# A pool of seven PSUM banks for the second attention of a two-attention layer

## The reference, cut to what matters

```python
def _mha(xq, xk, xv, Wq, bq, Wk, bk, Wv, bv, Wo, bo, causal):
    q = jnp.einsum('bsd,hde->bhse', xq, Wq) + bq[None, :, None, :]
    k = jnp.einsum('bsd,hde->bhse', xk, Wk) + bk[None, :, None, :]
    v = jnp.einsum('bsd,hde->bhse', xv, Wv) + bv[None, :, None, :]
    scale = 1.0 / jnp.sqrt(jnp.asarray(HD, q.dtype))
    scores = jnp.einsum('bhqe,bhke->bhqk', q, k) * scale
    if causal:
        ...
    w = jax.nn.softmax(scores, axis=-1)
    out = jnp.einsum('bhqk,bhke->bhqe', w, v)
    out = out.transpose(0, 2, 1, 3).reshape(out.shape[0], out.shape[2], D)
    return out @ Wo + bo
h = _mha(x, x, x, ..., causal=True)
out = _mha(h, encoder_k, encoder_v, ..., causal=False)
```

## Time and profile before

| | us |
|---|---|
| median of three runs | 3932.46 (3927.11 to 3933.49) |
| the profiled execution | 3969.99 |
| its span | 3968.2 |
| second attention, first scores to last unit | about 3451 to 3894 of the span |
| TensorE busy over the span | 3345.0 (84%) |
| DVE busy | 2614.8 (66%) |
| ACT busy | 1963.7 (49%) |

### The profile page before, as it was taken

The page is one execution under the profiler, slowest core; times in us unless marked ns, Lnnn a source line. Parts: engine busy times, 40 slices in busy tenths (PEclk is TensorE's granted clock), DMA queues, the critical chain, the costliest instruction groups (busy, mean ns, idle before and its releaser), DMA issues. The chain is left out here.

```text
span 3968.2 us, 96220 instructions
## 1 busy us (share of the span) xinstructions
PE 3345.0 (84%) x40498; PEld 2324.9 (59%) x40498; DVE 2614.8 (66%) x4510; ACT 1963.7 (49%) x3525; POOL 1266.7 (32%) x842
## 2 busy tenths in 40 slices
PE   7566797999999997756549668999999979999996
PEld 4445665777777776721123345766666656666664
DVE  5124375666666666279977778888888854666663
ACT  1122344555555554459950335665656652356552
POOL 1101303555555552400021336665556621000000
PEclk9577888999999998887878889999999995799996
DMA  1021401000000000800000221111111101000000
GB/s 40 6 63 57 157 1 39 1 10 1 10 1 1 1 1 20 274 28 1 1 5 2 62 71 32 53 49 45 44 53 38 30 15 39 9 19 20 11 1 11
DMA packets 88726, 131.40 MB, mean 33 GB/s; under 512 B 18450, under 2 KB 60106, under 8 KB 87532
## 3 DMA queue, kind: packets, MB, share of 16 engines
q1 hardware_dynamic: 85292, 119.03, 10.5%
q0 software_dynamic: 3008, 6.23, 0.4%
HBM read 86.63 MB, written 10.94 MB: 25 GB/s over the span
## 5 line engine op out<-in xcount | busy, mean ns | idle before, releaser
L2774 POOL TENSOR_TENSOR wide_probs<-wide_probs,wide_factor 128x1024 f32<-128x1024 f32 x128 | 239.6, 1893 | 311.1 <-ACT wide_factor L2735 311.1
L175 POOL TENSOR_TENSOR model_Y<-model_Y,model_X 128x512 f32<-128x512 f32 x12 | 15.2, 1266 | 963.7 <-POOLq L66 963.7
L2731 ACT ACTIVATE wide_probs<-wide_ps_s,wide_nm 128x1024 f32<-128x1024 f32 (+1 forms) x256 | 237.2, 926 | 172.5 <-DVE wide_nm L2816 152.8
L2281 ACT ACTIVATE narrow_probsT<-narrow_ps_t 128x512 f32<-128x512 f32 (+1 forms) x448 | 228.5, 565 | 181.5 <-PE narrow_ps_t L2185 178.8
L2811 DVE TENSOR_REDUCE wide_nm<-wide_ps_s 128x1 f32<-128x1024 f32 x128 | 155.9, 1219 | 193.6 <-PE wide_ps_s L2617 193.6
L3921 POOL TENSOR_TENSOR local_turn<-local_turn 128x1024 f32<-128x1024 f32 x96 | 226.7, 2368 | 158.7 <-DVE local_turn L3979 158.2
L2336 DVE TENSOR_REDUCE narrow_part<-narrow_ps_s 128x1 f32<-128x512 f32 x384 | 237.3, 682 | 57.9 <-PE narrow_ps_s L2168 57.9
L2185 PE MATMUL narrow_ps_t<-narrow_Q,second_KQ 32*128 32x256 f32 (+1 forms) x1664 | 261.8, 401 | 0.2 <-ACT narrow_probsT L2281 0.2
L3135 DVE TENSOR_TENSOR bonds_strain<-peri_in_moved 128x1664 f32<-128x1664 f32 (+3 forms) x128 | 257.0, 2083 | 1.0 <-PEq L66 1.0
L3186 PE MATMUL bonds_ps<-bonds_act_of,bonds_out 128*32 128x448 f32 (+3 forms) x1024 | 153.5, 696 | 117.9 <-ACT bonds_act_of L3159 83.9
L2629 PE MATMUL wide_ps<-model_ident,wide_probs 128*128 128x128 f32 (+1 forms) x1664 | 239.0, 274 | 10.8 <-DVE wide_probsT L2821 9.1
(11 more groups left out here) (643 smaller groups left out, 8433.9 us busy)
## 6 DMA issues: line engine op xcount, KB each, us to landing
moe_w<-in_L_ffn_w SPq DMA_DIRECT2D x62, 512.0 KB, 4.9
local_V<-local_V SPq DMA_DIRECT2D x96, 128.0 KB
e_wqkv<-in_L_ffn_qkv SPq DMA_DIRECT2D x6, 1536.0 KB, 6.8
local_V<-local_V SPq DMA_DIRECT2D x144, 64.0 KB
context_rows<-in_ctx SPq DMA_DIRECT2D x8, 768.0 KB
e_keys<-in_ctx_T SPq DMA_DIRECT2D x6, 800.5 KB, 4.9
e_source<-in_ctx_T SPq DMA_DIRECT2D x4, 800.5 KB, 4.5
second_source<-in_ctx_T SPq DMA_DIRECT2D x4, 800.5 KB, 6.4
```

What stands on the lines that cost most here:

```text
L2281: act.activation(probsT[0:high, c % PROBS, h, 0:wide], bank[0:high, 0:wide], ACT.Exp).then_inc(t_taken_act.sem, 1)
L2731: act.activation(probs[:, n % 2, h, lo:hi], ps_s[h][:, 0:hi - lo], ACT.Exp, bias=nm[:, n % 2, h, 2 * half:2 * half + 1], scale=1.0, accum_ ...
L2774: pool.tensor_tensor(v, v, factor[:, n // 4 % 2, j:j + 1].broadcast_to([P, CUT]), ALU.mult).then_inc(lowered[i].sem, 1)
```

## The change

The seven banks become one list. A loop ahead of the kernel walks the plan with assumed times (0.4 us per unit on TensorE, 1.2 for `times`, 2 us from issue to release, 0.6 per unit on DVE, 0.5 on ACT) and gives each unit the bank that it expects to be free first. Each unit waits for the last user of its bank, whichever engine empties that. The plan itself, the instructions and their operands' shapes are as before. Where `a.context` is false the banks and waits come out as before. At every place where a bank is asked for, `wait_bank_s` and `wait_bank_t` become `empty`, and `full_s` and `full_t` become `full`.

```diff
@@ narrow_attention: set-up, after the plan is sorted
     SB, TBK = 4, 3
+    BANKS = SB + TBK
+
+    slot_of, turn_of, last_in = {}, {}, {}
+    users = [[] for _ in range(BANKS)]
+    free, issued, dve_through, act_through = [0.0] * BANKS, 0.0, 0.0, 0.0
+    for e in plan:
+        if e[0] == "times":
+            issued += 1.2
+        if e not in s_rank and e not in t_rank:
+            continue
+        if a.context:
+            k = min(range(BANKS), key=lambda k: free[k])
+        else:
+            k = s_rank[e] % SB if e in s_rank else SB + t_rank[e] % TBK
+        issued = max(issued + 0.4, free[k])
+        if e in s_rank:
+            free[k] = dve_through = max(dve_through + 0.6, issued + 2)
+        else:
+            free[k] = act_through = max(act_through + 0.5, issued + 2)
+        slot_of[e], turn_of[e] = k, len(users[k]) + 1
+        last_in[e] = users[k][-1] if users[k] else None
+        users[k].append(e)
...
-        ps_s = [place.psum(f"ps_s{i}", [P, BANK]) for i in range(SB)]
-        ps_t = [place.psum(f"ps_t{i}", [P, BANK]) for i in range(TBK)]
+        ps = [place.psum(f"ps{i}", [P, BANK]) for i in range(BANKS)]
...
-        s_made = [place.counter(f"s_made{i}") for i in range(SB)]
-        t_made = [place.counter(f"t_made{i}") for i in range(TBK)]
+        bank_made = [place.counter(f"bank_made{i}") for i in range(BANKS)]
...
+        def empty(pe, e):
+            before = last_in[e]
+            if before in s_rank:
+                pe.wait_ge(s_taken.sem, s_taken.nth(s_rank[before] + 1))
+            elif before is not None:
+                side, nth = taken_t(before)
+                pe.wait_ge(side.sem, side.nth(nth))
+            return ps[slot_of[e]], bank_made[slot_of[e]]
+
+        def wait_made(engine, e):
+            engine.wait_ge(bank_made[slot_of[e]].sem, bank_made[slot_of[e]].nth(turn_of[e]))
+
+        def full(engine, e):
+            wait_made(engine, e)
+            return ps[slot_of[e]]
...
-                    bank, made = wait_bank_t(pe, e)
+                    bank, made = empty(pe, e)
```

More of the change, by code:

```diff
@@ L2136, in _ @@
                 elif kind == "value":
-                    bank, made = wait_bank_s(pe, e)
+                    bank, made = empty(pe, e)
                     c0, c1 = value_units[n]
@@ L2244, in _ @@
                 if kind == "ahead":
-                    bank = full_t(act, e)
+                    bank = full(act, e)
                     c0, c1 = AHEAD_UNITS[n]
@@ L2303, in _ @@
                 if kind == "value":
-                    bank = full_s(dve, e)
+                    bank = full(dve, e)
                     c0, c1 = value_units[n]
```

32 lines of the change are left out of this document (6 added, 26 removed).

## The result

Timed side by side, 19 runs each: before 3933.39 us median (3922.80 to 3971.23), after 3916.54 us (3901.56 to 3935.23). A later comparison of the same two kernels gave 0.9919 (0.9901 to 0.9936). The direction was right and the size was not.

The account below looks back on a forecast made before the run. No engine was full (TensorE 84%); in the second attention, units were taken to wait on bank releases by DVE and ACT. Gains 4.3 + 1.7 + 7.4 = 13.4 us, 13.3 of the median 3932.46, gave 3919 us, range 3909 to 3929.

Parts of the forecast that it names:

- Head, 4.3: Start of the second attention, only score units: seven banks instead of four keep DVE full, 4.3 us gained.
- the reductions' sum: Score units at the stage's start: DVE's idle gaps between reductions close, 2.25 + 1.08 + 0.45, sum 3.8 us.
- the upper bound of 4.8: Score units at the stage's start: at most 4.8 us if TensorE is also three units further ahead of DVE.
- The 0.5 of step 1: Step 1: a score unit held for DVE finds its bank long free; value units behind it come 0.5 us earlier.
- rival 1: Clock takes gains back: score units at the start 3.1, tail 5.7, middle 1.7 us; 3922 to 3927 us, chance 0.17.
- Middle, 1.7: Steps 2 to 14: 1.7 us gained in all, from the units before times 6; bounds -6 and +8.
- Stretch A: Units before times 3 in each middle step: DVE stays full, stays 5.77 us, cost 0.0, bound +0.6 per step.
- rival 2: Units before times 3: DVE's line hides nothing, nearer predecessors cost 21 us in all; 3940 us, chance 0.07.
- Stretch B: Units before times 5 in each middle step: one wait on "lift" passes to the turned unit behind, 0.0.
- Stretch C: Units before times 6: last turned unit's bank is released sooner, 0.14 us gained in each of thirteen steps.
- Tail, 7.4: After the last scores: all seven banks serve turned units instead of three, three blocks gain 2.35, 2.65 and 2.36 us.
- Sum, 13.4: Whole kernel: gains of the second attention's start, middle and tail added, 13.4 us of the profiled execution's 3969.99.

Follow-up runs that it names:

- the plain rotation: Changed kernel with the seven banks given out in simple turn in the second attention, no expected releases: 3912.98 us, 0.9928 of the kernel before.
- the head or the middle alone: Two kernels, each the kernel before with the new bank assignment only ahead of the first turned unit, or only from there to the last scores unit: 0.9977 and 0.9983.
- that with copies: Changed kernel with the last gather unit's copy on DVE made five times more: 0.9945 of the kernel before.

## Why the prediction was wrong

- **Head, 4.3.** The size was right, 4.5, and partly by luck. The value weights came 4.86 us sooner where the reductions' sum was 3.8; that is the upper bound of 4.8, TensorE's longer lead over DVE. The 0.5 of step 1 came as forecast (from its "lift" unit to the next value units 1.43 us for 1.91). Two terms that the sum didn't have ate it up: the clock rose 4.0 us behind the first value weights and not 3.2, which cost 0.3, and a turned unit then stood 0.64 us for ACT, which cost 0.5 (5.66 us for 5.17 up to the first times unit; the plain rotation has 5.17). The rise moved nearly with the work; rival 1's head, 3.1, did not come. That 3.1 was the bound of 4.8 less 1.7; from the 4.3 of the forecast it would have been 2.6.
- **Middle, 1.7.** Within 0.8: 2.5, with two of its three walks wrong. Stretch A was walked at 0.0 and became 5.85 from 5.77 us, since a score unit's start does slip far enough for DVE to stand 0.12 us; rival 2's mechanism exists, at an eighth of its price of 0.6. Stretch B, walked at 0.0, gave 0.16 (2.01 to 1.85). Stretch C gave 0.08 to 0.13 for the forecast 0.14. The errors have two signs, and that the sum came out near is luck.
- **Tail, 7.4.** The mechanism was right and the size too small: 9.4. The blocks came out at 3.40, 5.09 and 3.35 for the forecast 3.40, 5.24 and 3.36, so 7.5. The rest is the clock: the dip of 6.9 us that stood near 3868.5 between the blocks was gone, and the stretch from the second block to the third fell from 7.51 us (3871.85 to 3879.36) to 5.54 (3841.51 to 3847.05). I had the number, 9.1 if the dip went, and kept the dip because TensorE still stands for ACT.
- **Sum, 13.4: the failed step.** "Sum: 4.3 + 1.7 + 7.4 = 13.4 us of the profiled execution's 3969.99" has no term from outside the stage. The stage itself gave 16.4, ratio 0.9958 or 3916 us, inside the range. The sum put the code behind the stage at nothing without a reason. In the profiled executions it gave another 10.1 us, 74.8 to 64.7, though the change doesn't touch it, and which of the two it takes goes with the moment at which the stage ends. With 10.1 in two of three executions of the changed kernel, 16.4 + 6.7 = 23.1 us gives 0.9941; the measured are 0.9937 and 0.9919. What sets the clock's pattern, and so the share of each in the timed executions, stays open. I had weighed the clock only where work was edited (head and tail), and not the last digit of the earlier trace rows: 6, where its four neighbours are 9. That slice of 99 us holds the layer behind the stage.
- **Rivals.** None ended below 3913, so none of them held the measured 3907.7. Rival 1 had the right mechanism with one sign only: a clock that takes back. With the head or the middle alone it did take back (5.3 and 3.9 us of the tail).

The row that speaks most plainly of the clock is the 24.00 us before in which TensorE is busy for 23.40 at 0.50, that is 1.2 GHz. The Trainium skill ("TensorE: Matmul & The Clock Gate", "What's actually happening") says that the throttled state is the default and that activity releases it. By that rule the clock would rise within this dense stretch; the trace doesn't agree, and the measurement decides: in five executions (three with the old assignment, one of the changed kernel, one of that with copies) the clock stayed low through all of this work.

## What to carry to other kernels

Give PSUM banks out of one set when two consumers take turns: a stretch that one of them has alone then uses them all (5.75 to 3.40 us), and here a plain rotation did as well as a planner. Where everything hangs on the release of a bank, as in this tail, a block's time follows from its banks and its consumer's pace, and could be worked out to 0.2 us ahead of the run. But cut the traces at the same instructions before crediting a change, and price each stretch of low clock up to the end of the program, also in layers that aren't touched: here 10 of the profiled 26 us were there.

## What the runs showed of the hardware

- The same code takes 63.8 to 64.8 or 74.5 to 74.8 us, by whether the clock is at 2.4 or 1.2 GHz in its down projection (14.45 or 25.55 us); 1.5 us of added copies ahead of it exchanged one for the other.
- The granted clock stayed at 1.2 GHz through 24.00 us in which TensorE was busy for 23.40, and on to the end of the span.
- A pair of groups of eight matmuls (128x128 and 128x1) takes 3.41 us at 1.2 GHz and 1.78 at 2.4, from start to start: 1.9 times.
- Two executions of the kernel before reach the same instruction 24 us apart (3451.0 and 3426.6), with stages that agree to 0.1 us. The changed kernel's three stages are 425.97, 426.21 and 422.74: the clock can move a stage too.
- A 1.3 to 1.5 us longer stage (442.4 to 443.7 and more), by copies or by another assignment, went with 64.4 to 64.7 us behind it in place of 74.8.
